# Windowed attention in four fused layers: the weighted sums go through ScalarE to SBUF, and five steps change their slot

## What is computed

```python
h = ln(x)                                    # layer 0: over a whole image; else per token
h = windows(roll(h, (-3, -3)))               # (windows, 49, 96)
q, k, v = heads(h @ wqkv + bqkv)
attn = softmax(q * hd**-0.5 @ k.T + bias + mask)
o = (attn @ v) @ wp + bp
x = x + roll(windows_back(o), (3, 3))
x = x + gelu(ln(x) @ w1 + c1) @ w2 + c2      # layer 3: one more ln before w2
```

## Time and profile before

| | |
|---|---|
| median of 3 runs | 8194.28 us |
| the profiled execution | 8198.08 us |
| its span in the trace | 8196.3 us |
| granted TensorE clock, mean | 0.992 of full speed |
| busy: PE / DVE / POOL / ACT | 94% / 74% / 65% / 60% |
| PE's share of the chain that ended last | 68% |

### The profile page before, as it was taken

The page is one execution under the profiler, slowest core; times in us unless marked ns, Lnnn a source line. Parts: engine busy times, 40 slices in busy tenths (PEclk is TensorE's granted clock), DMA queues, the critical chain, the costliest instruction groups (busy, mean ns, idle before and its releaser), DMA issues.

```text
span 8196.3 us, 312040 instructions
## 1 busy us (share of the span) xinstructions
PE 7699.8 (94%) x109686; PEld 5836.7 (71%) x109686; DVE 6095.8 (74%) x18297; ACT 4936.6 (60%) x8745; POOL 5289.4 (65%) x6553
## 2 busy tenths in 40 slices
PE   5999999999899999999989999999999999999998
PEld 3677777767667777776767777777776677777777
DVE  6777778767777777876777677776687778778677
ACT  3746647557674765745767475574576647566457
POOL 4856656556785665656778465564678856566566
PEclk9999999999999999999999999999999999999999
DMA  1101101010010110101011011010101101011010
GB/s 60 37 11 28 50 13 31 11 33 17 24 37 30 32 46 17 31 7 39 11 30 37 30 32 41 21 31 7 40 5 34 56 10 30 14 25 29 11 39 24
DMA packets 309909, 227.60 MB, mean 28 GB/s; under 512 B 217379, under 2 KB 305766, under 8 KB 306344
## 3 DMA queue, kind: packets, MB, share of 16 engines
q1 hardware_dynamic: 307858, 215.98, 9.8%
q10 hardware_dynamic: 1622, 6.13, 0.2%
HBM read 117.62 MB, written 104.37 MB: 27 GB/s over the span
## 4 chain that ended last, share of the span: by engine, by line
PE 68%; DVE 14%; issue 9%; DVEq 3%; ACT 3%; POOL 2%; POOLq 0%; ACTq 0%; DMA 0%; SPq 0%
PE ps L932 11%; PE ps L992 11%; PE ps L893 8%; PE ps L1035 7%; PE ps L1008 7%; PE ps L917 7%; PE ps L939 5%; PE ps L962 3%; PE ps L972 3%; DVE bst L1061 3%; DVE S L1259 2%; PE ps L981 2%; ACT PT L797 2%; DVE xn L1210 2%; PE ps L1022 2%
## 5 line engine op out<-in xcount | busy, mean ns | idle before, releaser
L657 POOL TENSOR_TENSOR S<-S,mx 113x588 f32<-113x588 f32 (+1 forms) x2048 | 2065.8, 1009 | 1369.6 <-DVE mx L1261 1368.2
L797 ACT ACTIVATE PT<-ps 123x490 f32<-123x490 f32 (+1 forms) x2048 | 1061.5, 518 | 1088.3 <-PE ps L992 1082.5
L1259 DVE TENSOR_TENSOR S<-ps,bias 113x588 f32<-113x588 f32 (+1 forms) x1536 | 959.2, 624 | 744.5 <-PE ps L917 743.6
L1261 DVE TENSOR_REDUCE mx<-S 113x12 f32<-113x588 f32 (+1 forms) x2048 | 1359.9, 664 | 71.0
L780 ACT ACTIVATE S<-S 113x588 f32<-113x588 f32 (+1 forms) x2048 | 1249.2, 610 | 269.3 <-POOL S L657 257.8
L992 PEld LDWEIGHTS ps<-turn,S 113*123 113x123 f32 (+2 forms) x8704 | 965.6, 162 | 493.7 <-issue 304.2
L992 PE MATMUL ps<-turn,S 113*123 113x113 f32 (+2 forms) x8704 | 1270.4, 271 | 8.4 <-ACT S L780 6.2
L1008 PEld LDWEIGHTS ps<-w,G 128*98 128x98 f32 x12288 | 1150.4, 167 | 159.3 <-issue 87.5
L932 PEld LDWEIGHTS ps<-Va,PT 123*49 123x49 f32 (+1 forms) x18432 | 825.2, 125 | 497.4 <-issue 403.5
L1008 PE MATMUL ps<-w,G 128*98 128x96 f32 (+1 forms) x12288 | 1151.3, 250 | 0.0
L932 PE MATMUL ps<-Va,PT 123*49 123x27 f32 (+1 forms) x18432 | 984.8, 207 | 166.3 <-ACT PT L797 98.5
(11 more groups left out here) (94 smaller groups left out, 12002.7 us busy)
## 6 DMA issues: line engine op xcount, KB each, us to landing
v_between<-Vd SPq DMA_DIRECT2D x384, 165.4 KB
Va<-v_between SPq DMA_DIRECT2D x768, 41.3 KB
Vb<-v_between SPq DMA_DIRECT2D x768, 27.6 KB
v_between<-Vd SPq DMA_DIRECT2D x128, 153.1 KB
Vl<-v_between SPq DMA_DIRECT2D x256, 76.6 KB
out_dram<-x SPq DMA_DIRECT2D x15, 1176.0 KB
x<-x_dram SPq DMA_DIRECT2D x14, 1176.0 KB
mask<-mask_dram SPq DMA_DIRECT2D x258, 37.5 KB
```

The costliest lines, as they stand in the source:

```text
L657: pool.tensor_tensor(v, v, m, ALU.subtract).then_inc(a_sub, 1)
L797: act.activation(PT[0:rows, (s + 3) % 4, 0:blocks, :].rearrange("p b q -> p (b q)"), ps[0:rows, PT_BANK, 0:blocks * PAIR], ACT.Copy).then_ ...
L1259: dve.tensor_tensor(dst, scores, b, ALU.add).then_inc(a_bi, 1)
L1261: dve.reduce_max(mx[:, e, 0:nh], S[:, e, 0:n].rearrange("p (h k) -> p h k", k=N), axis=AX.X).then_inc(a_mx, 1)
```

## The change

PE, in slot 3, waits for a new semaphore `a_oc` and no longer for `a_o` before it writes pair 0 to `O_BANK`, and transposes the next input (L981) before it transposes `Ot` (L972). ACT gets a copy in slot 2, from the bank to a new SBUF tile `Os`, which sets `a_oc`; DVE's reciprocal and multiply wait for that and read `Os`. The rest is moved: ACT's three key copies (one, one, one in slots 0, 1 and 2, behind the exponential; in layer 3 its one key copy goes from slot 1 to slot 0), ACT's `hT` copy (from the end of slot 3 to behind the exponential), DVE's aggregation (slot 1 to slot 3), POOL's centring and scaling (slots 1 and 2 to slot 0, on both sides of the subtraction) and POOL's statistics and power (slot 0 to slot 2).

```diff
# POOL, attend
+                        if s == 0 and l > 0 and on(2): 
...
                         if on(0):
                             wait(a_mx, i.pair(s))
...
-                        if s == 0 and on(-3):
+                        if s == 2 and on(-3):
                             done = i - 3
                             wait(a_agg, done)
...
-                        if s == 2 and l > 0 and on(2):
+                        if s == 0 and l > 0 and on(2):
                             wait(a_xc, i + 2)
# ACT, attend
+                        if s == 2 and on(-1):
+                            wait(a_pv, i - 1)
+                            if on(-2):
+                                wait(a_o, i - 2)
+                            wide = QUAD * (C + nh)
+                            act.activation(Os[:, 0:wide], ps[0:TOK, O_BANK, 0:wide], ACT.Copy).then_inc(a_oc, 1)
                         if s == 2 and nh == 12 and on(1):
                             key_slot(2).then_inc(a_ke, 1)
# PE, attend
                             if s == 3:
-                                wait(a_o, i - 1)
+                                wait(a_oc, i - 1)
# DVE, attend
                         if s == 2 and on(-1):
-                            wait(a_pv, i - 1)
-                            outs = Ops.rearrange("p j h n -> p (j h) n")
+                            wait(a_oc, i - 1)
+                            outs = Os[:, 0:QUAD * (C + nh)].rearrange("p (m n) -> p m n", n=dh + 1)
                             dve.reciprocal(rec[:, 0:QUAD * nh], outs[:, :, dh]).then_inc(a_rec, 1)
...
                             stats(i - 2, xb, (i - 2).index * QUAD, QUAD, t, a_bn)
+                        if s == 3 and on(-2):
                             aggregate(i - 2, QUAD, t, a_bn, a_agg)
```

More of the change, by code:

```diff
@@ L222, in build @@
         rec = sb("rec", [TOK, QUAD * 12])
+        Os = sb("Os", [TOK, QUAD * 12 * 9])
         Ot = sb("Ot", [TOK, QUAD, C])
@@ L262, in build @@
             "bias_masked", "scores_done", "biased", "max_ready", "sub_ready", "exp_ready", "PT_done", "PT_ready"))
+        a_oc = sem("outputs_copied")
         a_pv, a_rec, a_o, a_ot, a_ote, a_y, a_res = (sem(n) for n in (
@@ L678, in attend @@
                                                ALU.subtract).then_inc(a_xc, 1)
-                        if s == 2 and l > 0 and on(2):
+                        if on(0):
+                            wait(a_mx, i.pair(s))
+                            v = S[:, s % 2, 0:n].rearrange("p (h k) -> p h k", k=N)
+                            m = mx[:, s % 2, 0:HEADS[l]].unsqueeze(2).to_broadcast([TOK, HEADS[l], N])
+                            pool.tensor_tensor(v, v, m, ALU.subtract).then_inc(a_sub, 1)
+                        if l == 0 and s == 3 and i.static and i.index == NQ - 1:
+                            image_rstd(g, 1, 0)
+                        if s == 2 and on(-3):
+                            done = i - 3
+                            wait(a_agg, done)
+                            stand(pool)
+                            pool.tensor_copy(mv[:, bass.ds(done.index * QUAD, QUAD), :],
+                                             agg[:, (j + 1) % 2, :, :]).then_inc(a_mv, 1)
+                            if l > 0:
+                                wait(a_mv, done)
+                                token_rstd(Unit(done.index * QUAD, None), 2 * l - 1)
+                        if s == 0 and l > 0 and on(2):
                             wait(a_xc, i + 2)
@@ L770, in attend @@
                         has_prior = on(-1) if s == 0 else on(0)
-                        if s == 1 and on(1):
+                        if has_prior:
+                            wait(a_sub, prior)
+                            act.activation(S[:, e, 0:nh * N], S[:, e, 0:nh * N], ACT.Exp).then_inc(a_exp, 1)
+                        if s == 0 and on(1):
                             wait(a_k, i + 1)
@@ L777, in attend @@
                                                ACT.Copy).then_inc(a_ke, 1)
-                        if has_prior:
-                            wait(a_sub, prior)
-                            act.activation(S[:, e, 0:nh * N], S[:, e, 0:nh * N], ACT.Exp).then_inc(a_exp, 1)
+                        if s == 1 and nh == 12 and on(1):
+                            key_slot(1)
                         if s == 1 and on(1):
@@ L799, in attend @@
                                 ps[0:rows, PT_BANK, 0:blocks * PAIR], ACT.Copy).then_inc(a_pte, 1)
-                        if s == 3 and on(2):
-                            wait(a_t1, i + 2)
-                            act.activation(hT[0:C, :, :, :].rearrange("p j w n -> p (j w n)"), turned_at(l, i),
-                                           ACT.Identity, bias=gb[:, l, 1:2],
-                                           scale=gb[:, l, 0:1]).then_inc(a_ht, 1)
                 mwait = waits(act)
@@ L964, in attend @@
                             last.then_inc(a_v, 1)
-                        if s == 3 and on(-1):
-                            if i.static and not on(0):
-                                busy(1, 1)
-                            wait(a_o, i - 1)
-                            if on(1):
-                                wait(a_vd, i + 1)
-                            for p in range(QUAD):
-                                last = pe.transpose(ps[0:C, Z_BANK, PAIR * p:PAIR * p + TOK], Ot[:, p, :], turn[:, :])
-                            last.then_inc(a_ot, 1)
                         if s == 3 and on(2):
@@ L983, in attend @@
                             last.then_inc(a_t1, 1)
+                        if s == 3 and on(-1):
+                            if i.static and not on(0):
+                                busy(1, 1)
+                            wait(a_o, i - 1)
+                            if on(1):
+                                wait(a_vd, i + 1)
+                            for p in range(QUAD):
+                                last = pe.transpose(ps[0:C, Z_BANK, PAIR * p:PAIR * p + TOK], Ot[:, p, :], turn[:, :])
+                            last.then_inc(a_ot, 1)
                         if on(-1) if s == 0 else on(0):
@@ L1211, in normed @@
                                              ALU.subtract, ALU.mult)
-                Ops = outputs_of(nh)
                 def enter():
```

23 lines of the change are left out of this document (5 added, 18 removed).

## The result

The changed kernel takes 8087.75 us (median of 4 runs, 8082.93 to 8087.89), the kernel before beside it 8195.24 us (8190.55 to 8197.31): a ratio of 0.9868, 95% interval 0.9851 to 0.9885, or 107.5 us less. 8095 was predicted. The profiled execution's span is 8086.1 us.

The account below looks back on a forecast made before the run. PE was taken to bound the kernel, waiting before L932 in slot 3. Gains of 0.27, 0.10, 0.10 and 0.35 us (layers 0 to 3) make 0.82, times 124 = 102 us off 8196.3; forecast 8095, range 8020 to 8290.

Parts of the forecast that it names:

- The chain, step by step: Slots 2 and 3, layers 0 to 2: from slot 2's scores (L917) to L972 takes 4.43 us, both slots 5.47.
- The wait that goes: PE's idle time before L932 in slot 3 vanishes in all layers; printed worth 1.87 us for one quad of each layer.
- The wait that comes: PE in slot 3 now waits some 0.5 us before L972, the transposes of `Ot`, ended by DVE's `Vd` line.
- The meeting with POOL: DVE's multiply L1273, now with two SBUF inputs, waits for POOL's subtraction in slot 2 and ends 0.41 us after it.
- Slots 0 and 1: Earlier exponential and subtraction give PE back 0.10 us a quad in layers 0 to 2, between 0 and 0.3.
- Layer 3: Multiply meets only the subtraction's end; 0.35 us a quad gained with slots 0 and 1, between 0.2 and 0.5.
- The sum: All layers: 0.82 us gained for one quad of each layer, times 124, is 102 us.
- The meeting costs nothing: Rival: DVE's multiply isn't slowed beside POOL, so 2.27 x 124 = 281 us are gained, 7913 us; chance 0.12.
- POOL goes first twice: Rival: layer 0's multiply also lets POOL's L664 and L641 pass, chain some 1.5 us longer, 8277 us; chance 0.16.
- The late exponential: Rival: slot 3's late bias delays the exponential before the next slot 0's transposes (0.1 us slack), 8185 us; chance 0.15.

## Why the prediction was right

**The chain, step by step.** From the rows of after, layer 1:

| step | predicted | after |
|---|---|---|
| slot 2's scores to DVE's bias | 0.62 | 1443.94 - 1443.33 = 0.61 |
| bias to maximum | 0.78 | 0.80 |
| maximum to POOL's subtraction | 0.84 | 0.85 |
| the subtraction | 1.17 | 1.17 |
| its end to the multiply's end | 0.41 | 0.42 |
| to the end of `Vd` | 0.46 | 0.47 |
| to PE | 0.15 (0 to 0.29) | 1447.79 - 1447.65 = 0.14 |
| sum | 4.43 | 4.46 |
| with the two groups behind | 5.47 | 1448.79 - 1443.33 = 5.46 |

**The wait that goes** went in front of the weighted sums, in all layers, and the copy took 0.51 against the 0.53 taken. **The wait that comes** is where it was put, with the size it was given (0.45 between starts of groups; "some 0.5 us"), and with `Vd` as its end. **The meeting with POOL** was the deciding step. It came from two lines of other shapes, 0.11 us and a difference of two durations, and held to 0.01. It holds wherever the two meet: the multiply ends 0.41 or 0.42 us after the subtraction in all 496 quads of the changed kernel in which they overlap, in all 496 with the aggregation back and in all 376 with `Vd` first, though it starts anywhere between 0.11 and 0.84 us after the subtraction's start. The Trainium skill's rule in SBUF — State Buffer, section "Who interferes with whom", that a DVE instruction with two SBUF inputs contends with a GpSimd instruction that reads SBUF, stands confirmed: 0.55 with one SBUF input, 1.10 with two, beside the same POOL instruction.

**Slots 0 and 1.** In layer 1 they take 10.93 - 5.46 = 5.47, and took 11.01 - 5.47 = 5.54: 0.07 gained, 0.10 predicted. In layer 0, 300.96 - 295.42 = 5.54 against 11.34 - 5.64 = 5.70: 0.16 gained, 0.10 predicted; slots 2 and 3 there gained 0.18 against 0.17. The 0.10 was taken for both, between 0 and 0.3, and one fell short as the other went over.

**Layer 3**: 0.36 against 0.35, and here luck helped. The prediction took away the printed 0.25 and set no new wait against it. Between starts of groups, over some 15 quads, 0.42 us went in front of L932's group and 0.18 came in front of the transposes of `Ot`, which with smaller shifts leaves 0.24; the value projection gave 0.10. And the gain isn't the copy's: the moves alone bring layer 3 to 7.59, as the change does to 7.61.

**The sum** is 0.34 + 0.08 + 0.08 + 0.36 = 0.86 for one quad of each layer where 0.82 stood, times 124 = 107 us where 102 stood; 107.5 was measured. The mechanism of layers 0 to 2 is shown; that the sum is so close is in part luck: the terms were off by 0.01 to 0.07 us a quad, in both directions.

**The rivals.** The meeting costs nothing (7913): the multiply's 1.10 excludes it. Its price was near: the kernel with the reciprocals in PSUM in layers 0 to 2 takes the meeting away and runs 7926. POOL goes first twice (8277): layer 0's rows exclude it; the multiply ended 0.41 after the subtraction, beside L676, which had started at 304.34. (Its price was added up a little high: 1.2 - 0.55 is 0.65 and not 0.67, 2 us less.) The late exponential (8185), ACT and then PE in layer 1, at the transposes of the next slot 0:

```profile
1450.40 0.69 ACT L775 ACTIVATE S<-S 113x588 f32<-113x588 f32 x1 [0.93 <-POOL S L669]
```

```profile
1451.24 0.73 PE L1000 MATMUL ps<-turn,S 113*123 113x113 f32 x5
```

The exponential ends at 1451.09 and the transposes start 2.45 us after slot 0's scores (1448.79), just as before (1446.65 - 1444.20), and without idle time. So it didn't decide, but it was close: the exponential ended 7.76 after slot 2's scores where 7.67 was predicted, and 0.15 before PE used it, which is the step that the prediction allowed.

**What the prediction had, and what it didn't see.** It priced the change as it stands, and the numbers held. Where the gain comes from it told only by half. It read the copy as what takes 1.87 us of waits away, and gave the moves 0.10 a quad and cover for the rest. The runs turn that round: the moves without the copy gain 219 us, and the copy without the moves loses 657, some 430 of it by the clock. The step "slots 0 and 1" contained that: the same early bias and maximum that shorten the chain to `Ot` would also have shortened the wait at L932, had DVE read PSUM as before. That sum wasn't made, since the change doesn't leave the copy out.

## What to carry to other kernels

Before an operand goes from PSUM to SBUF to free a bank early, look at what the reader's other operand is and what GpSimd does at that moment: here a VectorE multiply whose two inputs were both in SBUF ended 0.4 us after GpSimd's subtraction, whenever it had started, while with one input in PSUM it went through at full speed. Then put the small operand in PSUM, if a bank has room (135 us here), or let an instruction that reads PSUM go first (120 us). And undo the parts of a change one at a time: the copy in the title cost 110 us until the meeting was taken away and brought 51 after that, and of the moves that bring 219 us together, four cost 438 when each is undone alone.

## What the runs showed of the hardware

- A VectorE multiply of 113x384 took 0.55 us with one input in PSUM beside GpSimd's subtraction, and 1.10 (layer 1), 1.17 (layer 0) or 1.27 (with the aggregation in front) with both in SBUF. What differs is how long the subtraction still had to run. It got in at the end of the GpSimd instruction under way even when another followed without a gap, and that next one then took longer: GpSimd's copy of 98x8 (L676) has a median of 0.52 us in the changed kernel and 0.19 with the reciprocals in PSUM. A VectorE copy in the earlier trace rows had not got in: it ended only with the next GpSimd instruction. Why the two differ wasn't tried.
- TensorE's granted clock fell from 2.4 to 1.2 GHz in all eight passes through layer 3 of the two kernels with the copy and no moves, where PE stood 0.7 to 0.9 us in one piece in front of the transposes of `Ot`, once per quad of 8.0 to 8.45 us. The fall came within 0.4 us of the end of such a wait. The length of the wait alone doesn't decide it: in quads of 11 us and more PE stood 0.83 to 0.86 us (the change without the swap) or, in nearly every quad, 1.24 us (the copy alone) in layer 0, and the clock held in every such pass that was traced but one of the latter kernel. And shorter waits can do it: it fell in one of the four traced passes of the kernel with GpSimd's steps back through layer 3, 0.2 us after a wait of 0.45; in the other three, with quads of 8.07 and waits of 0.52 and 0.32 in turn, it held. The price is large: 12.89 or 13.14 us for a quad of 8.3. What exactly decides it these runs don't settle.
- The idle time printed in front of a group of matmuls told less than the distance between starts of groups: 0.31 us printed in front of L990, 0.45 lost.
